# Normalising the next group's keys later on VectorE in a one-core attention layer

## The reference, cut to what matters

```python
def _rmsnorm(t, w):
    inv = rsqrt(mean(t * t, axis=-1) + EPS)
    return t * inv * w
xn = _layernorm(x)
q, k, v = heads(xn @ Wq.T), heads(xn @ Wk.T), heads(xn @ Wv.T)
q, k = _rmsnorm(q, q_norm_w), _rmsnorm(k, k_norm_w)
scores = q @ k.T / sqrt(HD) + slope * rel        # causal
s = (softmax(scores) @ v) @ Wo.T
g = silu(xn @ W.T + bias + lora(xn))
return x + s * g
```

## Time and profile before

| | us |
|---|---|
| median of 3 runs | 2694.29 |
| lowest and highest | 2690.87, 2695.27 |
| the profiled execution, its own time | 2691.18 |
| its span in the profile | 2689.4 |
| TensorE busy in it | 2591.1 (96%) |
| VectorE, ScalarE, GpSimd busy | 1648.2, 1771.1, 1705.5 |

### The profile page before, as it was taken

One profiled execution on the slowest core, in us unless ns is written; L12 is line 12 of the kernel. 1 busy time (PEld: TensorE's weight loads), 2 busy tenths in 40 slices (PEclk: granted clock), 3 DMA queues, 4 the chain that ended last, 5 costly groups with the idle time before them and its releaser, 6 DMA issues.

```text
span 2689.4 us, 39881 instructions
## 1 busy us (share of the span) xinstructions
PE 2591.1 (96%) x13840; PEld 2297.7 (85%) x13840; DVE 1648.2 (61%) x3530; ACT 1771.1 (66%) x4635; POOL 1705.5 (63%) x835
## 2 busy tenths in 40 slices
PE   5689999999999999999999999999999999999997
PEld 4578888888888888888888888888888888888886
DVE  6446566657667556566566666556666755655666
ACT  4366666666776667667767667666767666666763
POOL 3377877876667656656667656565666756655653
PEclk9899999999999999999999999999999999999999
DMA  7888788775445333433335433433334533333323
GB/s 259 269 269 281 240 266 263 256 259 190 128 145 174 109 119 100 154 111 104 110 106 183 133 117 104 154 105 106 112 108 136 180 110 106 118 110 118 111 69 129
DMA packets 179192, 418.45 MB, mean 156 GB/s; under 512 B 31152, under 2 KB 72240, under 8 KB 178096
## 3 DMA queue, kind: packets, MB, share of 16 engines
q1 hardware_dynamic: 177728, 414.78, 47.4%
q10 hardware_dynamic: 1264, 1.12, 0.1%
HBM read 343.48 MB, written 89.13 MB: 161 GB/s over the span
## 4 chain that ended last, share of the span: by engine, by line
PE 89%; DVE 3%; ACT 2%; DMA 2%; POOL 1%; issue 1%; SPq 1%; POOLq 0%; DVEq 0%; ACTq 0%
PE proj L486 21%; PE proj L488 21%; PE proj L487 21%; PE tr L581 5%; PE sc L486 3%; PE sc L487 3%; PE sc L488 3%; PE ot L487 3%; PE tr L561 3%; PE ot L488 3%; PE ot L486 3%; PE tr L554 1%; DMA wu<-xtok 1%; SPq L313 1%; DVE acc L1226 1%
## 5 line engine op out<-in xcount | busy, mean ns | idle before, releaser
L985 POOL TENSOR_TENSOR wl<-wl,wh 128x896 fp32r<-128x896 f32 x436 | 948.9, 2206 | 608.7 <-ACT wh L740 608.6
L486 PE MATMUL proj<-wh,xh 128*128 128x448 f32 x1792 | 673.8, 376 | 25.0 <-POOL wl L985 17.5
L487 PE MATMUL proj<-wl,xh 128*128 128x448 f32 x1792 | 661.1, 369 | 0.0
L488 PE MATMUL proj<-wh,xl 128*128 128x448 f32 x1792 | 661.1, 369 | 0.0
L996 POOL TENSOR_TENSOR wb_lo<-wb_lo,wb_hi 128x1024 fp32r<-128x1024 f32 x128 | 307.2, 2400 | 315.6 <-ACT wb_hi L750 315.6
L807 ACT ACTIVATE misc<-misc,negmax 128x128 f32<-128x128 f32 (+3 forms) x512 | 286.8, 565 | 250.2 <-DVE negmax L1202 250.2
L486 PE MATMUL proj<-o_hi,wb_hi 128*128 128x512 f32 x1024 | 424.9, 415 | 9.3 <-issue 6.1
L1226 DVE TENSOR_TENSOR acc<-acc,proj 128x512 f32<-128x512 f32 x480 | 327.7, 684 | 156.6 <-PE proj L488 155.3
L786 ACT ACTIVATE pT_hi<-tr 128x512 fp32r<-128x512 f32 (+3 forms) x512 | 197.3, 440 | 334.5 <-PE tr L581 334.5
L740 ACT ACTIVATE wh<-wl 128x896 fp32r<-128x896 f32 x436 | 395.5, 966 | 33.0 <-DMA wl<-wu 32.5
L488 PE MATMUL proj<-o_hi,wb_lo 128*128 128x512 f32 x1024 | 404.6, 395 | 0.0
(11 more groups left out here) (125 smaller groups left out, 4366.6 us busy)
## 6 DMA issues: line engine op xcount, KB each, us to landing
wl<-wu SPq DMA_DIRECT2D x436, 448.0 KB, 3.9
wb_lo<-wo_in SPq DMA_DIRECT2D x128, 512.0 KB, 3.3
wu<-xtok SPq DMA_DIRECT2D x13, 1792.0 KB, 10.2
wo_in<-wo SPq DMA_DIRECT2D x32, 512.0 KB, 6.0
xtok<-wa SPq DMA_DIRECT2D x52, 256.0 KB, 4.6
wu<-xtok SPq DMA_DIRECT2D x13, 896.0 KB, 5.6
gate_dram<-misc SPq DMA_DIRECT2D x32, 256.0 KB, 5.1
xtok<-xT SPq DMA_DIRECT2D x28, 256.0 KB, 5.1
```

The lines of the kernel that those rows point to most:

```text
L486: pe.matmul(out, hi_l, hi_r, start=first, stop=False, skip_group_check=onto)
L487: pe.matmul(out, hi_l, lo_r, start=False, stop=False, skip_group_check=onto)
L488: return pe.matmul(out, lo_l, hi_r, start=False, stop=last, skip_group_check=onto)
L985: pool.tensor_tensor(w_slot(wl, w), w_slot(wl, w, True), w_slot(wh, w), ALU.subtract).then_inc(w_ready, 1)
```

## The change

The normalisation of the keys leaves the end of step 2 and goes into step 3, behind the first two score maxima and directly ahead of the normalisation of the first queries. Nothing else is changed, and nothing is added or left out.

```diff
@@ step(n, j) on VectorE @@
                 score_max(m, 0)
                 score_max(m, 1)
                 if j == 3 and more:
+                    scale_rows("k")
                     scale_rows("q0")
                 score_max(m, 2)
                 score_max(m, 3)
@@
                 for k in range(3):
                     probs_lo(m, k)
-                if j == 2 and more:
-                    scale_rows("k")
                 if j == 1:
                     gate_product(n)
                 add_out(v, 2)
```

## The result

The changed kernel took 2677.24 us (median of 6 runs, 2674.51 to 2681.06), the kernel before 2693.91 (median of 6, 2690.87 to 2695.27): a ratio of 0.9942, 95% interval 0.9930 to 0.9953. The profiled executions differ by 14.6 us: 2674.8 us of span against 2689.4.

The account below looks back on a forecast made before the run. The prediction took TensorE, busy 96% of the span, to bound the kernel. New waits of 7.0 us less 13.1 us removed gave -6.1 us, from 2694.29 to a median of 2688.2 us, range 2681 to 2697.

Parts of the forecast that it names:

- What bounds the kernel: Whole kernel: TensorE, busy 96% of the span, sets the time, plus the few places where it stands still.
- why the six steps were late: Step 3, groups 0, 1, 3, 5, 13, 21: GpSimd held the keys' normalisation, delaying maximum 0 for score tile 2.
- The term removed, 13.1 us: Six held groups: step 3 loses its excess over 21.20 us, 13.1 us together, 10.1 if the clock drops come anyway.
- The new place of the keys: Step 3 behind maximum 1: keys held until 0.55 us after GpSimd's pair, just in time for TensorE's transposes.
- The order of the two waiters: When the keys let go, VectorE's queries go before GpSimd's bias and end 0.61 us after the keys.
- The sum of new waits, 26 x 0.25 + 0.5 = 7.0 us: TensorE at the queries' transposes in step 3: 0.25 us in 26 groups, 0.5 in group 6, 7.0 us added.
- 0.1 us for a broken chain: TensorE at the queries' transposes: about 0.1 us more than the 0.18 us wait, so 0.25 a group was taken.
- Case B: No new wait at the queries' transposes, only group 6's 0.5 us: -12.6 us, 2681.7 us; chance 0.12.
- Case C: GpSimd's bias gets in between keys and queries, TensorE waits 0.7 us in 26 groups: +6.1 us, 2700.4; chance 0.13.
- Case D: The gain was luck of one execution, with half of the 13.1 us: about 0 change, 2694.8 us; chance 0.20.

Follow-up runs that it names:

- e7: Kernel before with GpSimd making the next step's bias ahead of the pair of low weight parts at the end of step 2; 2733.31 us, ratio 1.0169.
- e4: Kernel before with one empty instruction on TensorE ahead of the four pieces of step 3; ratio to before 0.9996.
- e2: Changed kernel with VectorE waiting for the end of the keys before issuing the queries; 2690.06 us, 1.0003 of before.
- e1: Changed kernel with the keys' normalisation left out in the 31 groups, an empty instruction in its place; 2675.84 us, ratio to before 0.9946.
- e8: Changed kernel with an empty reciprocal on its own tile between keys and queries; 2689.09 us, 0.9998 of before.
- e9: Changed kernel, code unchanged, timed again in turn with the kernel before on one chip; 2678.94 us against 2691.25, ratio 0.9949.
- e10: Changed kernel with TensorE waiting in steps 0 and 1, ahead of the pieces, for its last transpose but four; ratio to before 0.9946.
- e3: Kernel before with the keys' normalisation moved ahead of the third low part of the probabilities in step 2; 2681.83 us, 0.9968 of before.
- e5: Changed kernel with TensorE waiting in steps 0 and 1, ahead of the pieces, for its own last transpose; ratio to before 0.9988.
- e6: Kernel before with TensorE waiting in step 3, ahead of the pieces, for its own last transpose; ratio to before 1.0023.

## Why the prediction was wrong

- **What bounds the kernel, and why the six steps were late: right.** The waits went where named, groups 6 and 12 were rightly left out as ScalarE's (group 6 waited again, 1.39 us, and its step took 0.53 us more, where 0.5 was put; group 12 did not wait, against the forecast, but 20 and 24 did, 0.6 us each), and e7 showed the price of held keys in nearly every group.
- **The term removed, 13.1 us: right** (13.3 in the profile, both half-clock stretches included). How much of it another execution of before has to give is partly luck: e4's trace has 11.0.
- **The new place of the keys: right in every time.** Held behind GpSimd's second low part, 2.29 us in most groups, ready as TensorE asks; the queries 0.6 us behind; the bias behind both. The order of the two waiters, read from a single place, held in all 31 groups, and e2 showed what it is worth.
- **The sum of new waits, 26 x 0.25 + 0.5 = 7.0 us: this is the step that failed.** The wait of 0.18 us is there, but I added it to a step whose rest I took as fixed. The pieces behind it ran at 204.4 ns a matmul in place of 208.3, which gave back 0.18 us: the ordinary steps 3 took 21.16 to 21.23 us, where 21.4 to 21.5 were forecast, and the term was worth nothing there. The "0.1 us for a broken chain" was not paid either: the first piece began 0.18 us later and no more. e1 (no wait, no gain from it) and e2 and e8 (a longer wait at full price beyond the first 0.2 us) fix this. So do the groups of before that had the fast cadence already (2, 4, 7, 15 and 23, 21.00 to 21.03 us): with the wait they took 21.16 to 21.19, since there was nothing to give back. Both cadences thus stood in the trace of before, beside the 21.20 us of group 9; I had not asked why. Without this term the sum is -12.6 to -13.1 us, where 14.6 were measured between the traces.
- **Case B** came nearest (2681.7), with the wrong reason: the wait was not hidden, it was repaid. It stood at the edge of the range, which left nothing for the scatter between executions below it.
- **Case C** did not come. e2 showed its price to be right; the bias then held the queries for 0.27 us (0.95 in place of 0.68), far from its whole 1.56.
- **Case D** was half right: which of groups 1 to 5 are held differs between executions, but in the three traces it was never fewer than three, and groups 0, 13 and 21 were held in each, so the gain doesn't vanish.
- **What stays open:** the 14.6 us between the two profiled executions are 11.0 in step 3 and 3.6 elsewhere (1.2 before the first group, 1.5 in the last one, 0.8 in steps 0 to 2 of the others). No run ties the first two to the change; the time before the first score tile was 95.7 to 99.2 us in the traces, without a pattern. Of steps 0 to 2 something may belong to it: nine steps 0 of the changed kernel have the fast cadence, 0.17 us each, and none of before. In the traces with late queries in step 3 (the changed kernel's, e2, e8, e9, e10) it was 4 to 9, in before, e1, e3, e4 and e7 none. Why is open, and so is what sets the cadence at all.

## What to carry to other kernels

Where VectorE and GpSimd share work in SBUF, look for VectorE operations with two SBUF inputs that sit close to the start of a GpSimd operation: which of them waits is decided by a tenth of a microsecond, and the one to move is that behind which the critical engine's input is queued. Put such operations where being held is harmless rather than where they usually are not, and keep neighbours of this kind side by side, without a wait or another operation between them. When a sum adds a small new wait to an engine that is always busy, look first whether the work behind it has one cadence or two.

## What the runs showed of the hardware that was not expected

- A chain of 448-column matmuls at full granted clock ran at two cadences: behind the first interval of 0.29 to 0.31 us, 206.5 or 202.7 ns from start to start (208.3 and 204.4 with the first interval counted in). In step 3, without a wait for the queries ahead of it, mostly the slow one (132 of 155 steps); behind a wait of some 0.2 us or more for the queries always the fast one (153 of 153); behind TensorE's wait for its own last transpose fast in 73 of 82 steps (e5 and e6). The pieces of step 2 nearly always ran at 202.7 ns, in both kernels. What sets the cadence was not found.
- GpSimd's bias, a `tensor_scalar` of 1.56 us, held VectorE for only 0.23 us (e8) to 0.46 us (L1147, L1150). With the bias's own 1.56 us counted back from its end, VectorE went on 0.53 to 0.55 us behind its start in each of these places (an estimate from the earlier trace rows and the rows of e7 and e8). Its `tensor_tensor` of 2.1 us held VectorE until 0.13 us before its recorded end.
- A waiting GpSimd got in between two VectorE operations with two SBUF inputs when a wait or a one-input operation stood between them, and in none of the 31 groups when nothing did.
